# Recurrent scan with a mixture of experts beside it: products without readers fill the half steps, input products are moved, and GpSimd makes a high part

## The reference, cut to what matters

```python
def step(h, xs):                      # xs = x @ W_z, x @ W_r, x @ W of this step
    z = sigmoid(xzt + h @ U_z + vz)
    r = sigmoid(xrt + h @ U_r + vr)
    hh = tanh(xht + r * h @ U + vh)
    return (1 - z) * h + z * hh       # 128 steps, one after the other
...
sh = gelu(einsum('td,sdh->sth', xf, sW1) + sb1)      # 2 shared experts, hidden 512
shared = einsum('sth,shd->std', sh, sW2) + sb2
gates = xf @ rW + rb                                 # top 2 of 8 routed experts
h = gelu(einsum('td,edh->eth', xf, W1) + b1)
y = einsum('eth,ehd->etd', h, W2) + b2
```

## Time and profile before

| what | us |
|---|---|
| three timed runs | 987.19, 992.68, 992.14, median 992.14 |
| the profiled execution, its own time | 999.38 |
| its span, first to last instruction | 997.6 |
| mean granted TensorE clock of the span (1 is 2.4 GHz) | 0.792 |
| scan, first tanh of r to last | 12.9 to 450.8 |

### The profile page before, as it was taken

The page is one execution under the profiler, slowest core; times in us unless marked ns, Lnnn a source line. Parts: engine busy times, 40 slices in busy tenths (PEclk is TensorE's granted clock), DMA queues, the critical chain, the costliest instruction groups (busy, mean ns, idle before and its releaser), DMA issues. The chain is left out here.

```text
span 997.6 us, 16031 instructions
## 1 busy us (share of the span) xinstructions
PE 794.5 (80%) x4605; PEld 714.2 (72%) x4605; DVE 571.0 (57%) x2227; ACT 537.6 (54%) x1554; POOL 307.4 (31%) x346
## 2 busy tenths in 40 slices
PE   5799999999998989898858886798882598988700
PEld 4688998988888888887847775687872477767500
DVE  3455455444466656767737764735454476767448
ACT  2344444444444766766747774544331388777645
POOL 0011111111111011111155435105664146645673
PEclk9996556566665989998969996878775699999955
DMA  8200049100003354555646721101111423220053
GB/s 264 80 16 17 16 115 269 47 16 17 17 27 110 130 179 139 191 174 177 201 148 199 255 67 35 54 4 41 44 40 35 115 87 112 80 77 16 27 152 104
DMA packets 104037, 97.13 MB, mean 97 GB/s; under 512 B 13564, under 2 KB 94781, under 8 KB 100110
## 3 DMA queue, kind: packets, MB, share of 16 engines
q1 hardware_dynamic: 89372, 76.84, 24.9%
q0 software_dynamic: 8704, 16.59, 5.4%
q10 hardware_dynamic: 5874, 2.68, 1.0%
HBM read 32.46 MB, written 33.37 MB: 66 GB/s over the span
## 5 line engine op out<-in xcount | busy, mean ns | idle before, releaser
L719 POOL DMA_INDIRECT moe_rows<-raw,pos_all x64 | 63.3, 990 | 377.2 <-DVE pos_all L1190 332.7
L1111 DVE TENSOR_TENSOR g_all<-g_f,g_all 128x256 fp32r<-128x256 f32 x312 | 129.5, 420 | 53.1 <-ACT g_all L994 34.9
L992 ACT ACTIVATE g_f<-bank,vecT 128x256 f32<-128x256 f32 x192 | 91.9, 478 | 32.5 <-remote 16.6
L342 PE MATMUL bank<-g_all,w_all 128*128 128x256 f32 (+1 forms) x288 | 107.0, 372 | 0.7 <-issue 0.4
L343 PE MATMUL bank<-g_all,w_all 128*128 128x256 f32 (+1 forms) x288 | 97.3, 338 | 0.0
L344 PE MATMUL bank<-g_all,w_all 128*128 128x256 f32 (+1 forms) x288 | 97.1, 337 | 0.0
L994 ACT ACTIVATE g_all<-bank,vecT 128x256 fp32r<-128x256 f32 x192 | 92.9, 484 | 0.0
L959 ACT ACTIVATE tr<-bank 128x32 f32<-128x32 f32 x128 | 25.3, 198 | 124.3 <-PE bank L778 120.9
L1954 POOL DMA_INDIRECT result_rows<-yrow,dest x80 | 81.3, 1016 | 20.7 <-issue 20.7
L2074 ACT ACTIVATE g_f<-bank,b1c 128x512 f32<-128x512 f32 (+1 forms) x96 | 59.5, 620 | 50.5 <-PE bank L344 44.2
L324 POOL DMA_INDIRECT slot_rows<-wide,posi x64 | 63.1, 986 | 67.2 <-DVE posi L1732 49.5
(11 more groups left out here) (378 smaller groups left out, 2419.7 us busy)
## 6 DMA issues: line engine op xcount, KB each, us to landing
dw<-w_all SPq DMA_DIRECT2D x20, 1024.0 KB
g_all<-w_all SPq DMA_DIRECT2D x10, 1024.0 KB
raw<-moe_rows SPq DMA_DIRECT2D x46, 128.0 KB
moe_out<-wide SPq DMA_DIRECT2D x46, 128.0 KB
slot_rows<-hs SPq DMA_DIRECT2D x8, 645.0 KB
result_rows<-hs SPq DMA_DIRECT2D x8, 512.0 KB
raw<-in_L_ffn_fc_w SPq DMA_DIRECT2D x16, 256.0 KB
x1T<-result_rows SPq DMA_DIRECT2D x16, 256.0 KB, 3.4
```

Source lines behind the costliest of these rows:

```text
L342: pe.matmul(out, a_hi, b_hi, start=start, stop=False, skip_group_check=True)
L719: gp.indirect_dma_start(out=moe_rows, out_offset=bass.IndirectOffsetOnAxis(ap=pos_all[:, i:i + 1], axis=0), in_=hrow[c % 2][:, k * P:(k + ...
L992: act.activation(gf(u), src, ACT.Gelu, bias=h1_bias(u), scale=0.5).then_inc(hidden_done, 1)
L1111: dve.tensor_tensor(glo(u), gf(u), ghi(u), ALU.subtract).then_inc(lo_done, 1)
```

## The change

Four edits. (1) `prefill(c + 1, 0)` goes from half 0 of chunk c + 1 to half 15 of chunk c, behind a wait on that chunk's last `hh` tanh; `prefill(c, 2)` goes from between the products for r and z to the end of half 0, behind a wait on its z tanh. The first chunk's z products go ahead of the scan. (2) `keep_clock` issues products of the identity with itself, 256 columns each, into the right half of the bank that the next unit takes; nothing reads them. They fill up a slot's count of products to 7 at odd halves and 3 at even halves; by the planner's tables that is 331 products: 69 in chunk 0, 34 in chunk 1, 22 in each of chunks 2 to 10, 19 in chunk 11, and 11 in chunks 12 to 15. (3) For the 168 units beside the scan ScalarE makes only `g_f`; GpSimd copies it to float32r (`high_part`), after `hidden_done`. `hidden_done` now counts 1 for such a unit. The four indirect DMAs of `spread` are dealt out over halves 10 to 13 of the next chunk between these copies; the last chunk's follow the scan. (4) `low_part` runs three slots after a unit's first layer on VectorE, not two, for all units, and waits for `hi_ready` too.

```diff
--- before.py
+++ after.py
@@ -206,6 +206,14 @@
 SHARED_SEEN = [sum(x[0] != "m" for x in PLAN.sums[:PLAN.sums.index(("s", c)) + 1]) for c in range(NCH)]
 
 
+def hi_on_act(u):
+
+    return PLAN.first_slot[u] >= PLAN.slot_of(NCH, 0)
+
+
+HIDDEN_DONE = [sum(2 if hi_on_act(v) else 1 for v in range(u + 1)) for u in range(NU0)]
+
+
 def w1_turns():
 
     out = []
@@ -690,6 +698,11 @@
 
             @block.gpsimd
             def _(gp):
+                def high_part(u):
+                    gp.wait_ge(hidden_done, HIDDEN_DONE[u])
+                    atleast(gp, l2_done, u - 5)
+                    gp.tensor_copy(ghi(u), gf(u)).then_inc(hi_ready, 1)
+
                 gp.memset(ident[:], 0.0).then_inc(ident_ready, 1)
                 gp.wait_ge(ident_ready, 1)
                 gp.affine_select(out=ident[:], in_=ident[:], compare_op=ALU.not_equal, fill=1.0, base=0,
@@ -706,19 +719,17 @@
                 last_row = gp.to_reg(MOE_ROWS - 1)
                 last_out = [gp.to_reg(OUT_ROWS[g] - 1) for g in range(2)]
 
-                def spread(c):
-
-                    n = c
-                    gp.wait_ge(hrow_ready, n + 1)
-                    gp.wait_ge(place_ready, n + 1)
-                    if n == 0:
-                        gp.wait_ge(filled, 32)
-                    for k in range(CT):
-                        for q in range(TOPK):
-                            i = (n * CT + k) * TOPK + q
-                            gp.indirect_dma_start(out=moe_rows, out_offset=bass.IndirectOffsetOnAxis(ap=pos_all[:, i:i + 1], axis=0),
-                                                  in_=hrow[c % 2][:, k * P:(k + 1) * P], in_offset=None,
-                                                  bounds_check=last_row, oob_is_err=False).then_inc(sent_h[c % 2], 16)
+                def spread(c, o):
+
+                    if o == 0:
+                        gp.wait_ge(hrow_ready, c + 1)
+                        gp.wait_ge(place_ready, c + 1)
+                        if c == 0:
+                            gp.wait_ge(filled, 32)
+                    i = c * CT * TOPK + o
+                    gp.indirect_dma_start(out=moe_rows, out_offset=bass.IndirectOffsetOnAxis(ap=pos_all[:, i:i + 1], axis=0),
+                                          in_=hrow[c % 2][:, o // TOPK * P:(o // TOPK + 1) * P], in_offset=None,
+                                          bounds_check=last_row, oob_is_err=False).then_inc(sent_h[c % 2], 16)
 
                 def gather(c):
 
@@ -741,8 +752,14 @@
                 gp.memset(zt, 0.0).then_inc(zt_ready, 1)
                 gp.wait_ge(zt_ready, 1)
                 gp.memset(zt.rearrange("p (n c) -> p n c", c=ROWW)[:, :, P:ROWW], FAR).then_inc(zt_ready, 1)
-                for c in range(NCH):
-                    spread(c)
+                for s in range(PLAN.slot_of(NCH, 0) + 2):
+                    if s - 1 in PLAN.first and not hi_on_act(PLAN.first[s - 1]):
+                        high_part(PLAN.first[s - 1])
+                    c, hf = events(s)
+                    if c is not None and 1 <= c < NCH and 10 <= hf < 10 + CT * TOPK:
+                        spread(c - 1, hf - 10)
+                for o in range(CT * TOPK):
+                    spread(NCH - 1, o)
                 gp.wait_ge(zeroed, 16 * 2 * E)
                 for c in range(NCH):
                     gather(c)
@@ -776,9 +793,6 @@
                     if hf == 0:
                         pe.wait_ge(h_ready, n + 1)
                         pe.matmul(half(bank[0], 0)[:, ts], uh[:, P:2 * P], last, start=False, stop=False, skip_group_check=True).then_inc(r_acc, 1)
-                        if t == 0:
-                            prefill(c, 0)
-                            prefill(c, 2)
                         pe.matmul(half(bank[1], 0)[:, ts], uh[:, 0:P], last, start=False, stop=False, skip_group_check=True).then_inc(z_acc, 1)
                         if t == STEPS - 1 and c + 1 < NCH:
                             pe.wait_ge(r_tanh, n + 1)
@@ -788,12 +802,31 @@
                         pe.wait_ge(z_tanh, n + 1)
                         pe.matmul(half(bank[1], 1)[:, ts], uh[:, 2 * P:3 * P], rh[:], start=False, stop=False, skip_group_check=True).then_inc(hh_acc, 1)
 
+                def next_chunk(c, hf):
+
+                    if hf == 2 * STEPS - 1 and c + 1 < NCH:
+                        pe.wait_ge(hh_tanh, STEPS * (c + 1))
+                        prefill(c + 1, 0)
+                        return 5
+                    if hf == 0:
+                        pe.wait_ge(z_tanh, STEPS * c + 1)
+                        prefill(c, 2)
+                        return 5
+                    return 5 if hf == 2 * STEPS - 2 and c + 1 < NCH else 0
+
+                def keep_clock(turn, n):
+
+                    if n > 0:
+                        w1_free(turn)
+                    for k in range(n):
+                        pe.matmul(half(bank[2 + turn % 3], 1), identr[:], identr[:].unsqueeze(1).broadcast_to([P, CT, P]), start=True, stop=True, skip_group_check=True)
+
                 def w1_free(turn):
 
                     if turn >= 3:
                         kind, i = W1_TURNS[turn - 3]
                         if kind == "u":
-                            pe.wait_ge(hidden_done, 2 * i + 2)
+                            pe.wait_ge(hidden_done, HIDDEN_DONE[i])
                         else:
                             pe.wait_ge(cols_ready, 2 * i + 2)
 
@@ -892,19 +925,28 @@
                 t.then_inc(setup_pe, 1)
                 pe.wait_ge(setup_dve, SETUP_DVE)
                 prefill(0, 1)
-
+                prefill(0, 0)
+
+                done, turn, now = 0, 0, (0, 0)
                 for s in range(PLAN.n):
                     if s in PLAN.scan:
                         scan_half(*PLAN.scan[s])
+                        done, now = 0, PLAN.chunk_half[s]
                     if s in PLAN.cols:
                         turn_rows(PLAN.cols[s])
+                        done, turn = done + CT, turn + 1
                     if s in PLAN.first:
                         first_layer(PLAN.first[s])
+                        done, turn = done + 3, turn + 1
                     if s in PLAN.second:
                         second_layer(PLAN.second[s])
+                        done += 3
                     if s in PLAN.back:
                         turn_back(PLAN.back[s])
+                        done += CT
                     c, hf = events(s)
+                    if c is not None and c < NCH:
+                        done += next_chunk(c, hf) + (CT if hf in (1, 3, 9) and c else 0)
                     if c is not None:
                         if c == 0 and hf == 2:
                             pe.wait_ge(small_in, NSMALL)
@@ -922,6 +964,8 @@
                             count(c - 1)
                         if c < NCH - 1 and hf == 9:
                             turn_x(c + 1)
+                    if s + 1 in PLAN.scan:
+                        keep_clock(turn, (7 if now[1] % 2 else 3) - done)
                     if s - 1 in PLAN.mix:
                         turn_mix(PLAN.mix[s - 1])
 
@@ -990,8 +1034,9 @@
                         t = DYN_JOBS.index(PLAN.units[u][1])
                         act.wait_ge(db_in[t % DW], 16 * (t // DW + 1))
                     act.activation(gf(u), src, ACT.Gelu, bias=h1_bias(u), scale=0.5).then_inc(hidden_done, 1)
-                    atleast(act, l2_done, u - 5)
-                    act.activation(ghi(u), src, ACT.Gelu, bias=h1_bias(u), scale=0.5).then_inc(hidden_done, 1)
+                    if hi_on_act(u):
+                        atleast(act, l2_done, u - 5)
+                        act.activation(ghi(u), src, ACT.Gelu, bias=h1_bias(u), scale=0.5).then_inc(hidden_done, 1)
 
                 def tile_sum(n):
                     kind, j = PLAN.sums[n]
@@ -1106,7 +1151,9 @@
                     dve.tensor_tensor(xs_lo[j % 2][:], src, xs_hi[j % 2][:], ALU.subtract).then_inc(cols_ready, 1)
 
                 def low_part(u):
-                    dve.wait_ge(hidden_done, 2 * u + 2)
+                    dve.wait_ge(hidden_done, HIDDEN_DONE[u])
+                    if not hi_on_act(u):
+                        dve.wait_ge(hi_ready, sum(not hi_on_act(v) for v in range(u + 1)))
                     atleast(dve, l2_done, u - 5)
                     dve.tensor_tensor(glo(u), gf(u), ghi(u), ALU.subtract).then_inc(lo_done, 1)
 
@@ -1338,8 +1385,8 @@
                         split_h(*PLAN.split[s])
                     if s - 1 in PLAN.cols:
                         columns(PLAN.cols[s - 1])
-                    if s - 2 in PLAN.first:
-                        low_part(PLAN.first[s - 2])
+                    if s - 3 in PLAN.first:
+                        low_part(PLAN.first[s - 3])
                     if s in PLAN.sum_ends:
                         summed(PLAN.sum_ends[s])
                     if s - 1 in PLAN.back:
```

## The result

Over four executions each the kernel before took 989.66 us (median; 983.59 to 992.68) and the changed kernel 925.32 us (919.83 to 934.25): ratio 0.934, 95% interval 0.926 to 0.941. On another chip six executions of the same changed kernel gave 0.932 (0.929 to 0.936). The profiled execution took 924.26 us, with a span of 922.5.

A forecast was written before the change was run, and what follows sets the result against it. The serial scan was taken to bound the kernel, its early steps slowed by TensorE's low clock (0.59). Savings 59 + 3.5 + 5.5 + 4 - 1 = 71 us took the 992.1 us median to 921; 8-in-10 range 901 to 957 us.

The forecast's parts named there:

- the case forecast (5): Whole kernel: the forecast itself, 921 us, with its own range 905 to 936 us; chance 0.65.
- chunks 1 to 10: Early scan: chunks fall from 26.2 to 20.3 us each with the clock mostly at its upper level, saving 59 us.
- chunk 0: First chunk, no units: two slow steps of 3.4 us, six of 2.3, 22 us in all, saving 3.5 us.
- chunks 12 to 15: Late scan: input products give 0.4 us a chunk, ScalarE's lost Gelu 0.6 a chunk; 4 us saved.
- SyncE's fill: Zero fill delays issuing chunk 7's input, which lands just in time; 1 us of loss booked.
- after the scan: From the scan's last tanh to the end: stays at 547 us, no change, all starts earlier.
- The clock: TensorE's granted clock from about 60 to 240 us: 0.85 or more, steps of 2.2 to 2.6 us.
- Rivals 1, 2 and 4: Clock stays low, 1022 us (chance 0.05); goes up and down, 950 us (0.17); fillers do nothing, within 0.5% (0.01).
- Fillers at the upper clock: Odd halves at 2.4 GHz: four products lie under the ScalarE and VectorE chain; 0.05 us a step booked.
- The copy: GpSimd's copy for units beside the scan: 0.6 us each, covered; at 1.4 us, 2 to 3 us on each late chunk.
- Ports: GpSimd's copy beside VectorE: nothing booked, bound 24 us over 80 steps; under the skill's exclusion rule 12 to 24 us worse.
- Rival 3: GpSimd holds VectorE up, by its length or the port, at the upper clock: 12 to 30 us lost, 940 us; chance 0.12.

The follow-up runs named there:

- run without lone fillers: Changed kernel without fillers where a slot's count lacks only one product (ten, nearly all in chunks 12 to 15): 919.26 us, 0.933 to the kernel before.
- scatter later: Changed kernel with GpSimd's scattering DMAs of chunks 0 to 7 moved to half steps 2 to 5 of the chunk after next: 0.941 to the kernel before.

## Why the prediction held, step by step

The forecast was 921 us, 71 us saved, and the median 925.3, 64 us saved; the case forecast (5) came true. Its sum, term by term, from the profiled executions:

| term | forecast saving | measured |
|---|---|---|
| chunks 1 to 10 | 59 | 51.2 (26.2 to 21.0 a chunk) |
| chunk 0 | 3.5 | 0.4 |
| chunk 11 | 5.5 | 3.6 |
| chunks 12 to 15 | 4 | 8.1 |
| SyncE's fill | -1 | inside chunk 6: -3.8 |
| after the scan | 0 | 12.2, mostly chance |

The total is better than its terms. Chunks 0 to 11 gave 12 us less than forecast, SyncE's 1 us counted, the late ones 4 more, and part of the closeness is luck. Chunks 1 to 10 came 8 us short: chunk 7 takes 19.2 us, under the 20.3 forecast, but chunks 2 to 4 (21.8) have the stall of the last step, and chunks 6 and 10 (23.0, 23.6) a fall of the clock. Chunk 0 had four slow steps (4.33, 3.52, 3.41, 4.42 us) where two were taken; in executions where the clock rose sooner it takes 19.6 to 21.1 us. Chunk 11 took 26.7 us on the other chip, as forecast.

**The clock, right.** 0.96 in the early scan and steps of 2.15 us. That the fillers hold the clock up is shown by leaving them out: at 1.2 GHz again, the product 415 ns. That they need the other edits for it, above all in chunks 2 to 4, the kernel with fillers only shows (0.70 over 60 to 145 us); the prediction gave the fillers the whole of it. By the Trainium skill (TensorE: Matmul & The Clock Gate, What's actually happening) the lower clock is the default state and activity releases it; the trace of the kernel without fillers agrees as to the default, with nine chunks of ten wholly at 415 ns a product. The rule doesn't tell this case from its opposite, though: TensorE is 99% busy there by the profile, and the clock stays down. Rivals 1, 2 and 4 are out.

**Fillers at the upper clock, right.** 0.05 us a step was booked and nothing is seen at 2.16 us. What the prediction left out is the wait that goes with them. It looked at the products' 0.13 us each and not at `w1_free` in front of them: 0.8 us twice a chunk from 12 on.

**The copy, its effect mis-sized.** L704 has a median of 0.40 us (mean 0.45), nearer the memset than the 0.6 taken:

```profile
L704 POOL CAST g_all<-g_f x168: 395/404/629, 44.8 to 390.2; 128x256 fp32r<-128x256 f32 x168
```

But ScalarE's relief was booked at 0.6 us a late chunk and at nothing in the early ones. The run with both Gelu back on ScalarE is slower by half of the gain, 3.3%, most of it in the early chunks, where the clock is up less of the time. How much of that is ScalarE's relief and how much that kernel's stall of the seventh step (counted from one) is open. That the fillers' banks come free one Gelu (0.476 us) later there is argued, not shown, as the reason. The term was missed because the prediction added the parts one by one; 25 us for fillers alone and a loss of 8 us for the rest alone make 51 together. The later low part and the dealt-out DMAs were never undone by themselves.

**Late chunks.** 4 us were forecast and 8.1 came, 10 on the other chip. The change without its fillers gave 94.8 - 82.1 = 12.7 in chunks 12 to 14, and lone fillers took 4.5 to 7 of them.

**SyncE, right in kind, too small.** "Just in time", 1 us, was a wait of 1.58 us, and the clock fell behind it: chunk 6 took 3.8 us more than chunk 7.

**Ports.** Nothing was booked and some 5 us came; one of the prediction's own signs of being wrong, chain operations of VectorE over 0.19 us, did appear. VectorE's zhh operation in the changed kernel (mean 220 ns over the scan, 193 before), the same with no copies on GpSimd, and a copy beside the h operation in the run without lone fillers:

```profile
L1120 DVE SCALAR_TENSOR_TENSOR zhh<-tz,hh x128: 172/192/455, 16.0 to 389.3; 128x32 f32<-128x32 f32 x128
```

```profile
L1120 DVE SCALAR_TENSOR_TENSOR zhh<-tz,hh x128: 181/192/198, 16.1 to 438.6; 128x32 f32<-128x32 f32 x128
```

```profile
93.71 0.41 POOL L704 CAST g_all<-g_f 128x256 fp32r<-128x256 f32 x1
93.72 0.46 DVE L1123 SCALAR_TENSOR_TENSOR h<-kept,zhh 128x32 f32<-128x32 f32 x1
```

An operation of 0.19 us takes 0.46 when it starts 0.01 us after the copy. The excess is 0.027 x 128 = 3.5 us for zhh and 1.7 us for the new h, 5.2 us together; 0.9 of them are one operation of 1.08 us beside three copies. On the other chip it is 4.5 us. Half of the longer zhh operations stand beside an indirect DMA and not beside a copy, but in the kernel without copies, which has the same DMAs, none is over 198 ns. The rule of the Trainium skill (SBUF — State Buffer, Who interferes with whom) that the two exclude each other for a whole instruction agrees with the rows of the copy and the h operation; the 12 to 24 us did not come because the copy mostly falls where VectorE waits, as argued. Rival 3 came true in kind, for about a fifth of the 24 us that the prediction took as its upper bound.

**After the scan.** The stretch from the last tanh of r to the end is 546.8 us in the profile of before, 538.0 in another execution of it (985.66 us), 534.6 and 551.1 in two of the changed kernel, and 533.0 to 547.6 in the others. So the 12 us between the first two profiles are not the change's as far as these executions can tell, and the median moved by 64 us, about what the scan gave (62.9).

## What to carry to other kernels

Where TensorE looks full, read a product's own duration before the busy share: it may be full because it is slow, and products without readers that lie under another engine's chain can pay for themselves. Place them behind the product that the chain waits for, and never behind a wait that the next product of the chain doesn't need. Edits that free an engine and edits that raise the clock don't add up; run them together and one by one.

## What was not expected of the hardware

- TensorE can be 99% busy by the profile and stay at the lower clock: in the kernel without fillers it is busy 141.2 of the 142 us from 58 to 200 us, and each product of L351 takes 415 ns there (a median of 283 at the upper level). The granted clock shows nothing of it, since the trace's first record is the rise at 229.9 us.
- A wait of TensorE of 1.1 to 1.6 us can be followed by a fall of the clock that costs 2.5 to 6 us more, and needn't: in chunk 6 it fell behind waits of 1.58, 1.46 and 1.44 us and not behind one of 1.25; after the stall at step 3 with the scatter later, it fell in chunks 5, 7 and 8 and stayed up in chunks 6 and 9.
- The stall of ScalarE beside GpSimd's indirect DMAs, 1.0 to 1.5 us in four chunks of the changed kernel, follows the DMAs when they are moved. Its mechanism is open.
